# A one-core kernel of attention, experts and Mamba: the second pass one turn behind, ones by GpSimd, stacks from two queues, a new order table

## What is computed

```python
x = x + 0.5 * ffn_ref(layernorm(x), ...)       # first pass, "a"
x = x + mamba_ref(layernorm(x), ...)           # Mamba-2, then an MLP of 512
x = x + 0.5 * ffn_ref(layernorm(x), ...)       # second pass, "b", same weights

def ffn_ref(x, ...):                           # n_head = 16, head size 8
    x = x + attn(x)     # layernorm, causal conv of 3, qkv, rotary, causal softmax, proj
    x = x + moe(x)      # layernorm, argmax router, 4 experts: silu(gate) * value @ proj
    return x
```

## Time and profile before

| | us |
|---|---|
| median of the runs (2) | 1726.17 |
| lowest, highest | 1722.39, 1729.95 |
| the profiled execution | 1728.04 |
| its span in the trace | 1725.9 |
| PE busy in it | 1412.1 |
| DVE, ACT, POOL busy | 1184.0, 803.5, 397.4 |
| mean granted TensorE clock | 0.89 |

### The profile page before, as it was taken

The page is one execution under the profiler, slowest core; times in us unless marked ns, Lnnn a source line. Parts: engine busy times, 40 slices in busy tenths (PEclk is TensorE's granted clock), DMA queues, the critical chain, the costliest instruction groups (busy, mean ns, idle before and its releaser), DMA issues.

```text
span 1725.9 us, 30393 instructions
## 1 busy us (share of the span) xinstructions
PE 1412.1 (82%) x11328; PEld 742.7 (43%) x11328; DVE 1184.0 (69%) x2807; ACT 803.5 (47%) x1266; POOL 397.4 (23%) x404
## 2 busy tenths in 40 slices
PE   1477889859989999889989898899898986985846
PEld 0133434435444445454544454455544453443323
DVE  5657484588589767868688768887796657655622
ACT  0153443533646545544555455555454553552422
POOL 0102132123131331205031403133221422221110
PEclk9678886978989999899989998999999898997867
DMA  5221300021202021121203031203011003003000
GB/s 181 37 39 27 45 1 18 18 37 26 30 28 43 21 45 40 30 33 45 44 26 44 29 50 35 35 22 58 21 35 28 29 24 54 13 14 54 25 17 23
DMA packets 75807, 61.43 MB, mean 36 GB/s; under 512 B 6800, under 2 KB 71824, under 8 KB 75664
## 3 DMA queue, kind: packets, MB, share of 16 engines
q1 hardware_dynamic: 71568, 51.10, 15.7%
q0 software_dynamic: 4096, 8.40, 1.6%
HBM read 19.23 MB, written 14.55 MB: 20 GB/s over the span
## 4 chain that ended last, share of the span: by engine, by line
PE 29%; DVE 11%; issue 5%; DMA 3%; SPq 3%; ACT 2%; POOL 1%; POOLq 0%; DVEq 0%; ACTq 0%
PE wring L743 5%; PE wring L550 4%; PE wring L748 3%; PE obank L596 3%; SPq L465 2%; DVE mx L1282 2%; PE aring L611 2%; PE aring L636 1%; DMA stq<-shiftT 1%; PE aring L653 1%; PE aring L576 1%; PE wring L756 1%; DMA stk<-low 1%; PE wring L762 1%; PE wring L858 1%
## 5 line engine op out<-in xcount | busy, mean ns | idle before, releaser
L921 ACT ACTIVATE prob_mem<-aring 128x1024 f32<-128x1024 f32 x320 | 324.9, 1022 | 188.7 <-PE aring L653 172.4
L1282 DVE TENSOR_REDUCE mx<-aring 128x2 f32<-128x1024 f32 (+2 forms) x384 | 317.5, 862 | 116.9 <-PE aring L636 105.0
L743 PE MATMUL wring<-wv,hb 128*128 x448 | 241.2, 648 | 18.3 <-ACT hb L958 12.7
L611 PE MATMUL aring<-ramps,spots 64*128 64x128 bf16 (+1 forms) x2560 | 179.3, 220 | 67.1 <-DVE mx L1282 26.9
L596 PE MATMUL obank<-prob_mem,vx 128*9 128x512 f32 (+3 forms) x2048 | 196.4, 484 | 12.3 <-ACT prob_mem L921 6.0
L611 PEld LDWEIGHTS aring<-ramps,spots 64*128 64x128 bf16 x2560 | 84.9, 97 | 275.3 <-issue 154.1
L1393 DVE SCALAR_TENSOR_TENSOR yv<-yv,wring 128x512 f32<-128x512 f32 x112 | 76.8, 685 | 110.2 <-ACT yv L963 109.6
L653 PE MATMUL aring<-stq,stk 50*128 50x512 bf16 (+3 forms) x1024 | 135.7, 325 | 0.0
L636 PE MATMUL aring<-stk,stq 48*128 48x512 bf16 (+3 forms) x1024 | 132.4, 320 | 0.0
L748 PEld LDWEIGHTS wring<-ep,yaT 128*128 128x128 f32 x896 | 112.6, 192 | 42.6 <-issue 42.0
L748 PE MATMUL wring<-ep,yaT 128*128 x896 | 125.6, 283 | 5.4 <-ACT yaT L873 5.0
(11 more groups left out here) (212 smaller groups left out, 2354.7 us busy)
## 6 DMA issues: line engine op xcount, KB each, us to landing
hb<-hd SPq DMA_DIRECT2D x16, 448.0 KB
stq<-high SPq DMA_DIRECT2D x96, 64.0 KB
stk<-high SPq DMA_DIRECT2D x96, 64.0 KB
stq<-mid SPq DMA_DIRECT2D x64, 64.0 KB
stk<-mid SPq DMA_DIRECT2D x64, 64.0 KB
od<-ob SPq DMA_DIRECT2D x16, 256.0 KB, 2.3
od<-ob SPq DMA_DIRECT2D x16, 192.0 KB, 2.1
x<-in_x SPq DMA_DIRECT2D x8, 256.0 KB
```

Source lines behind the costliest of these rows:

```text
L611: pe.matmul(dst, spots[rows, 2 * by_key + part, :], ramp, start=(part == 0), stop=False, skip_group_check=True)
L743: last = pe.matmul(ring[:], hTd[:, u * P:(u + 1) * P], wv[:, expert[u], o:o + DFF], start=True, stop=True)
L921: act.activation(prob_mem[:, k], ring[:], ACT.Exp, scale=float(HD) ** -0.5).then_inc(freed, 1)
L1282: last = dve.tensor_reduce(mx[:, j, h0 + q:h0 + q + 3:2], ring[:, :, c:c + w], AX_X, ALU.max)
```

## The change

Five edits:

1. `LAG` goes from 2 to 1: the second pass of row i stands in turn i + 1 and not in turn i + 2. There are 11 turns and not 12, and passes are numbered a0, a1, b0, a2, b1, ..., a7, b6, b7.
2. `ORDER` is new, of the same 1952 steps.
3. The ones of stk are no longer written by DVE in parts, but by POOL over both whole tiles (128 partitions x 4096 bf16), behind its other memsets; a new semaphore `setup_ones` tells SP and ACT.
4. x of row 0 is loaded ahead of the constants. Only row 1's x is loaded before the schedule; rows 2 to 4 follow in SP's queue behind the low pieces of the first front.
5. In the first front alone (n == 0) SP issues the q side's 12 stacks and ACT the k side's 12, each behind its own copies.

```diff
-LAG = 2
+LAG = 1
 
@@ sync block
-            for dst, src in loads:
-                sp.dma_start(dst[:], src).then_inc(s["const_loaded"], 16)
...
-                        for side in range(2):
+                        for side in range(2 if n > 0 else 1):
                             sp.wait_ge(ready, 2 * n + side + 1)
                             for product in (Q_ROWS, K_ROWS)[side][which]:
                                 stack(side, piece, product)
+                    if kind == "low" and n == 0:
+                        for later in range(2, XROWS):
+                            sp.wait_ge(s["x_loaded"], 16 * later)
+                            load(later)
...
             load(0)
+            for dst, src in loads:
+                sp.dma_start(dst[:], src).then_inc(s["const_loaded"], 16)
...
-            for row in range(1, XROWS):
-                sp.wait_ge(s["x_loaded"], 16 * row)
-                load(row)
+            sp.wait_ge(s["x_loaded"], 16)
+            load(1)
+            sp.wait_ge(s["setup_ones"], 2)
@@ scalar block
+            def stack_keys(piece, which):
+
+                for product in K_ROWS[which]:
+                    for a in range(2):
+                        first = HALF * a + HD * product
+                        act.dma_start(stk[0][1][first:first + HD, :, :],
+                                      piece[1][HALF * a:HALF * a + HALF, :]).then_inc(s["a_stacked"], 16)
...
+                        if n == 0:
+                            act.wait_ge(s["setup_ones"], 2)
+                            act.wait_ge(s["a_high"], 2)
+                            stack_keys(high, 0)
...
+                        if n == 0:
+                            act.wait_ge(s["a_mid_copied"], 2)
+                            stack_keys(midl, 1)
+                    elif kind == "low" and n == 0:
+                        act.wait_ge(s["a_low"], 2)
+                        stack_keys(low, 2)
@@ gpsimd block
+            pool.wait_ge(s["setup_rank"], EXPERTS - 1 + UNITS)
+            for k in range(2):
+                pool.memset(stk[k][1][:].rearrange("p h t -> p (h t)"), 1.0).then_inc(s["setup_ones"], 1)
@@ vector block
-            dve.wait_ge(s["setup_chain"], sc)
-            for a in range(2):
-                for k in range(2):
-                    step(dve.memset(stk[k][1][HALF * a + 32:HALF * (a + 1)], 1.0))
```

More of the change, by code:

```diff
@@ L158 @@
 ORDER = (
[L159 to L173, removed]
@@ L174 @@
-    "43245243422353325323025303230363333003030033043444444444334344413444114444441314444131441411315311133111311131"
-    "13311113331131111113131511311111311531131532323223323232026000000004444444444444444441111414141441411411414144"
-    "1514115111511111111151111111111111111112222222264444444444444444444444544444444555"
+    "00000000000011111111001110111111110111111111011111111111101111111121122212121221111116111111141114444141441444"
+    "44411441444444444445144451115111115333133331333331131313333331333313131331331233232232323323233333300000060004"
@@ new lines @@
+    "00440444440440404440141444114414454101441041414141111411115151111111511311311131111331313331331113313111113121"
+    "33123212323311232132331133113313311131131614114411414444141411144111411114441414411141114144124242323442332443"
+    "52332333300064000504045044404044404544440404004141141411041414414114011451441114115111111511115113113111311331"
+    "13333133113313111133311213122332313331212132311231133113116131113113111413411441111411441343411144413414443111"
+    "44114141431344242422332335204242406044500500040400444404445400414441010444114441014144411411151441144411115111"
@@ new lines @@
+    "11111055113111311131133131333331131133111112111231223132312131211323113133113313133131613134134141414444114144"
+    "11414113111144411441113143411341123242442423325423323300404404065000040444045404444450004401141141444441041144"
+    "41501414411144114111115111111111551131311131133131333313111331131113233123233233113212311213231133131113311131"
+    "11611341111444411414111411441443411144414144111311414113424434532332332342432402206440050000050444404404445004"
+    "14114411440410414144144114444141144111411515151011111151131311131111331031333331113133111113231131212123213321"
@@ new lines @@
+    "13213213131131113113116131111333114341111443411411114411431114341414144141424244432442442444323232333433500604"
+    "50450004040404404444504444004400414114141104141411414141401441511411111151115111151131311131133131333313111331"
+    "13111233113321322313331212123112331131133311311111613311141411444111441141441114114413111114114444124424242432"
+    "34423243245334343330600440044500440444054444444444454444454444414111151151111531131331311333333111113113133311"
+    "13311111133131111313311133311311132323223232322333333363334404440440444000044044444404444444444441511115115111"
@@ L177 @@
+    "1111111111151111111111111111111111111112222222264444444444444444444444544444444555"
 )
@@ L376, in build_program @@
             setup_chain const_loaded attn_w_loaded weights_loaded setup_weights setup_pool
-            setup_dve setup_act setup_dve2 setup_rank x_loaded out_stored a_link c_link b_link
+            setup_dve setup_ones setup_act setup_dve2 setup_rank x_loaded out_stored a_link c_link b_link
             a_mid_copied a_u a_var a_rstd a_hn a_cT a_rope a_high a_mid a_low a_stacked a_shift a_shiftT
```

## The result

The changed kernel takes 1968.18 us (median of two runs, 1956.67 to 1979.70) against 1726.17: a ratio of 1.139, 95% interval 1.126 to 1.152. Slower, as forecast, but by 242 us and not by 51, and outside the range. The profiled execution is the run of 1956.67.

The account below looks back on a forecast made before the run. The prediction took PE to bound the middle and chains the ends. Start to the end of row 0's second-pass core 425, six turns of 190.3 (1142), last row 140 and end 70 made 1777 us; range 1692 to 1835.

Parts of the forecast that it names:

- The setup: Before the first front: without DVE's four memsets the statistics start at about 10.6 us, 17.2 us earlier.
- It costs nothing: POOL's fill of two tiles in the setup: 4.2 to 8.4 us, done at about 11, hidden at no cost.
- C0a and row 0's chain: Row 0's first-pass core runs 49.3 to 111.7 us; its second-pass core starts 241 us later, at 352.7.
- Mamba leg: Row's chain from x combined to the Mamba result m_x: 127 us in row 0, 98 at shortest, 112 taken.
- C0b starting before 320: Sign of being wrong: row 0's second-pass core starting before 320 us would put the Mamba part near 98.
- The hole: Each turn's stretch without a core: about 10 us to m_x plus 45 of front, 55 us, PE busy 38.6.
- The two cores: Rest of a turn outside the hole, P: 129.7 us of PE work at 93% busy, 139.5 us.
- The loop: Turn T from a row's chain L and the cores' time P: T = (P + L) / 2 = 190.3 us.
- L: Chain from a row's first-pass core end to its second-pass core start: legs 84, 112 and 45, 241 us.
- Much slower: Rival: each leg stretches behind PE's queue, chain 259, turn 199, total 1829; upper part of the own forecast.
- The last row and the end: After the six turns: last row 140 us, taken between 119 and 153, and the end 70 as before.
- The faster rival: PE finds work everywhere, the hole costs nothing: turn 172.6 us at 97.5% PE, total 1671; chance 0.17.

Follow-up runs that it names:

- pool_ones: The kernel before with one edit, the ones of stk written by POOL and not by DVE: 1718.47 us, 0.9926.
- uncovered: The kernel before, LAG = 2, with 35 non-core steps pulled ahead of the second-pass core in five turns, fronts unmoved: 1880.84 us, 1.0865.
- holes_lag2: The kernel before, LAG = 2, second fronts of rows 1 to 5 moved behind the preceding core, with 35 non-core steps each: 1944.6 us, 1.1248.
- early_fronts: The changed kernel, second fronts of rows 0 to 6 reading a constant tile instead of the Mamba result and standing one core earlier: 1990.56 us, 1.1494.
- covered_lag1: The changed kernel with 10 to 17 expert steps (30 in the last) moved from each hole beside the second core: 2230.44 us, 1.2879.
- late_fronts: The kernel before, LAG = 2, with only the nine second-front steps of rows 1 to 5 moved right ahead of their core: 1899.92 us, 1.0975.

## Why the prediction was wrong, point by point

**The setup: right in kind, 5 us short.** DVE's memsets are gone and POOL's hide, as said. The statistics start at 11.80 and not at 10.6. The constants do come later, negA starts at 9.40 and not at 8.28; but the order of the loads isn't the cause of the 1.2 us, since pool_ones, with the constants first, also starts at 11.80. It is "It costs nothing" that failed: the first DVE operations ended only with POOL's fill, at 9.84. From the first stacking to the first mask it now takes 54.19 - 27.81 = 26.4 us, before 22.7. The second queue was taken at 0; the runs say 0 or a little worse. The rule of the Trainium skill (DMA: Bandwidth & Descriptors, "Issuing engines are not separate DMA queues") agrees with that: 1716.61 us with two queues, 1716.28 with one.

**C0a and row 0's chain: oversized.** C0a ends at 119 (111.7). Core end to C0b's start is 202 us (241): its Mamba leg was 80 and its first leg 81. The sign I had named, C0b starting before 320, was just missed (321.4), and what it stood for had come: the Mamba leg was even under 98.

**The hole: right in kind, 7 us short.** The front was a little quicker than the 45 us taken: 43 us from m_x to the next first mask in row 2, 37 to 44 in all rows, so the sign "45 us or more" in every turn didn't come, and three rows were even under the 40 that I had named as a sign of being wrong. But from the core's end to m_x it took 21 us in the mean of six turns and not 10. I had counted that in row 2 alone, where 14 steps lie between; in rows 1 to 6 it is 14 to 30 steps and 13 to 28 us. (The holes of the table are 52 to 74 steps, not 53 to 75.) The whole hole is 62.2 us in the mean, forecast 55 by PE and 51 by the loop. Two signs came, stronger than said: a clock of 0.87 in the middle, PE's share over the span at 0.77 (0.80). The m_x distances, forecast at 187 to 200, were 209.6, 227.4, 215.6, 229.9 and 229.1 us from row 2 on.

**The two cores: here the forecast failed.** "The other 129.7 us run in the two cores [...] I take 93% [...] That is P = 139.5 us". They took 225.3 - 62.2 = 163, 24 us more a turn: three quarters of the 31 between the 194.5 forecast by PE and 225.3. The step supposes that a core gives back in time what PE no longer has to do beside it. uncovered shows that it doesn't: 35 steps taken away, 34 us of hole, 4 back. In the changed kernel itself the two cores gave back 22 us a turn for a hole of 62. The rows were there: C6b, with 40 steps beside it, took 72 us, and the stretch before it 62; C2b after takes 76 and its hole 56. With these and a first core between those 72 and the 98.5 of before, at 85, a turn would have been 219. I read C6b's row for its 90% and not for its 72 us. A PE share is no floor: it holds busy time that a lower clock has lengthened, and leaves out what the core waits for itself.

**The loop: bookkeeping, wrongly fed.** With P = 163 and row 2's chain of 279, T = (P + L) / 2 gives 221, near the 225, as it must: L = T + hole and T = P + hole hold for any turn, by their definition. But L was fed with legs as they stand where little else runs, and the legs stretch with the turn: 81 and 80 us in row 0, 105 and 131 in row 2. holes_lag2 loses as much with no loop, and early_fronts cuts the loop and gains nothing: L followed from the table's order, and didn't set the time. "Much slower" named that stretching, but with P at 139.5 it too came to 1829 only.

**The last row and the end: right**, 140 and 69. The last row is 43 + 37 + 60, each part a little under the 48.5 + 43 + 62 read before; that the middle of 119 and 153 met it to the us is luck.

**The faster rival** said that no rule makes holes in the cores into holes in PE. Its answer is in uncovered: a hole full of steps keeps PE 86% busy, but the core that it was taken from leaves PE idle instead.

**Open.** How the 40 us a turn divide when the clock is held fixed: the accounts give 24 idle and 16 clock, yet a lower clock may also lengthen the waits. In covered_lag1 the cause is shown for the one wait of 10.1 us; that its other waits for the shift (113.9 us in 33 places from 394 to 1900 us) arise alike is not shown.

## What to carry to other kernels

Where a latency-bound stage runs with filler beside it, price a hole by its own length and the stage by its measured length with less filler, never by PE's busy share. Filler taken out of the stage can cost almost its full time alone and give back little: 4 us for a hole of 34 in uncovered, 10 for 39 in late_fronts, 22 for 62 in the changed kernel. And count the steps of every turn, not of one. Look for a stretch of the old trace in which the new arrangement stands already, and read its microseconds before its percentages. Here an order table that keeps each long chain under another row's core was worth more than a shorter distance between a row's stages. Every engine works through its own part of the table in order, so a step with a late input holds up the steps behind it: 6.6 us of DVE waiting for a gather became 10.1 us of PE waiting for a shift in covered_lag1.

## What the runs showed of the hardware

PE's work, busy time times granted clock, stayed within 1.2% (158.2 and 160.0 a turn) while the clock went from 0.94 to 0.87, so the clock alone lengthened the same matmuls by 16 us a turn. More PE activity raised it (0.845 to 0.898 over the span, by 116 us of dummy matmuls in the six turns), but gave back 56 us for the 116 or more. POOL fills 128x4096 bf16 in 3.48 us, as long as DVE needs for 32x4096: I had allowed 4.2 each. While POOL filled, small DVE operations (negA, 0.17 us before) took 0.44 to 1.21 us and ended together with the fill, at 9.84 in four kernels.
